# GpSimd's sums of x and output bias and the x2 store take other places in a fused cross-attention and expert kernel

## What is computed

```python
wq = (layernorm(x) @ wq_w.T + wq_b); wk = (ctx @ wk_w.T + wk_b); wv = (ctx @ wv_w.T + wv_b)
probs = softmax(einsum('bthd,bshd->bhts', wq, wk) / sqrt(16))
attn = einsum('bhts,bshd->bthd', probs, wv)
x2 = x + attn @ wo_w.T + wo_b
xt = layernorm(x2); xhat = layernorm(xt); top1 = argmax(xt @ Wg.T)
out = x2 + gelu((xhat * ln_scale[top1] + ln_bias[top1]) @ W1[top1] + b1[top1]) @ W2[top1] + b2[top1]
```

## Time and profile before

| | us |
|---|---|
| three runs, median | 1463.2 |
| lowest and highest run | 1460.85, 1465.98 |
| profiled execution, its own time | 1460.63 |
| its span, first to last instruction | 1458.4 |
| TensorE busy in the span | 1412.0 |
| VectorE busy | 1172.7 |
| ScalarE busy | 872.4 |
| GpSimd busy | 465.0 |

### The profile page before, as it was taken

One profiled execution on the slowest core, in us unless ns is written; L12 is line 12 of the kernel. 1 busy time (PEld: TensorE's weight loads), 2 busy tenths in 40 slices (PEclk: granted clock), 3 DMA queues, 4 the chain that ended last, 5 costly groups with the idle time before them and its releaser, 6 DMA issues.

```text
span 1458.4 us, 39587 instructions
## 1 busy us (share of the span) xinstructions
PE 1412.0 (97%) x15438; PEld 1206.9 (83%) x15438; DVE 1172.7 (80%) x2880; ACT 872.4 (60%) x1451; POOL 465.0 (32%) x602
## 2 busy tenths in 40 slices
PE   6899999999999999999999999989999999999998
PEld 5788888888888888888888888868888888888887
DVE  4788888888888888888888888777777777777775
ACT  5577776777777777777777677653343434333342
POOL 4223332232223223332323233223343434334340
PEclk8899999999999999999999999999999999999999
DMA  7566656665566556756675666412212222222211
GB/s 186 122 170 178 176 158 158 175 173 161 158 166 176 161 161 170 178 150 170 171 176 143 168 172 172 134 34 87 84 61 74 72 73 73 73 73 72 75 59 44
DMA packets 150480, 190.89 MB, mean 131 GB/s; under 512 B 17631, under 2 KB 101146, under 8 KB 150298
## 3 DMA queue, kind: packets, MB, share of 16 engines
q1 hardware_dynamic: 150298, 188.38, 47.5%
HBM read 53.01 MB, written 33.55 MB: 59 GB/s over the span
## 4 chain that ended last, share of the span: by engine, by line
PE 81%; DVE 14%; issue 3%; ACT 1%; DMA 0%; POOL 0%; SPq 0%; ACTq 0%; DVEq 0%
PE st_ps L1252 13%; PE s_ps L1233 12%; PE pp_ps L1110 9%; PE pp_ps L1083 7%; PE pv_ps L1058 7%; PE st_ps L1044 6%; PE s_ps L1016 6%; PE pp_ps L1118 6%; DVE negmax L747 6%; PE pv_ps L1066 4%; DVE cT_lo L773 3%; PE s_ps L1240 2%; PE pp_ps L1199 2%; DVE negmax_wide L750 2%; PE pp_ps L1104 2%
## 5 line engine op out<-in xcount | busy, mean ns | idle before, releaser
L747 DVE TENSOR_REDUCE negmax<-s_ps 128x8 f32<-128x1024 f32 x256 | 311.4, 1216 | 23.0 <-PE s_ps L1016 23.0
L594 ACT ACTIVATE pT<-st_ps 128x1024 f32<-128x1024 f32 x256 | 262.9, 1027 | 106.0 <-PE st_ps L1044 105.0
L1252 PE MATMUL st_ps<-w_hi,q_packed 128*128 128x256 f32 x1024 | 215.9, 296 | 0.2
L1252 PEld LDWEIGHTS st_ps<-w_hi,q_packed 128*128 128x128 f32 x1024 | 167.9, 189 | 10.3 <-issue 5.9
L472 POOL TENSOR_TENSOR xb<-xin,bo_all 128x256 f32<-128x256 f32 x128 | 90.8, 731 | 263.1 <-DMA x_scratch<-xb 170.6
L1233 PE MATMUL s_ps<-k_packed,w_hi 128*128 128x512 f32 x512 | 171.5, 423 | 0.6 <-ACT pT L648 0.6
L1016 PE MATMUL s_ps<-k_packed,q_packed 96*128 96x128 bf16 x2048 | 158.3, 220 | 9.7 <-DVE negmax L747 5.8
L460 POOL TENSOR_TENSOR q_parts<-q,q_parts 128x1024 bf16<-128x1024 f32 x32 | 68.5, 2140 | 298.2 <-ACT q_parts L588 298.2
L1044 PE MATMUL st_ps<-q_packed,k_packed 98*128 98x128 bf16 x2048 | 158.3, 220 | 0.0
L637 ACT ACTIVATE offhotT<-pv_ps 96x512 bf16<-96x512 bf16 x31 | 18.4, 592 | 222.9 <-PE pv_ps L1220 222.9
L1016 PEld LDWEIGHTS s_ps<-k_packed,q_packed 96*128 96x128 bf16 x2048 | 128.3, 98 | 27.8 <-DVE negmax L747 17.8
(11 more groups left out here) (181 smaller groups left out, 3492.9 us busy)
## 6 DMA issues: line engine op xcount, KB each, us to landing
q_packed<-q_parts SPq DMA_DIRECT2D x192, 256.0 KB, 3.9
k_packed<-k_parts SPq DMA_DIRECT2D x192, 256.0 KB, 4.4
xin<-in_x_dram SPq DMA_DIRECT2D x32, 512.0 KB, 3.9
cin<-in_ctx_dram SPq DMA_DIRECT2D x32, 512.0 KB, 4.0
x_scratch<-xb SPq DMA_DIRECT2D x32, 512.0 KB, 4.5
xin<-x_scratch SPq DMA_DIRECT2D x32, 512.0 KB, 3.9
out_dram<-xb SPq DMA_DIRECT2D x32, 512.0 KB, 2.9
q_packed<-negmaxT SPq DMA_DIRECT2D x128, 8.0 KB
```

The lines of the kernel that those rows point to most:

```text
L594: a.activation(pT[u % 2][:], st_ps[:], ACT.Exp, scale=DH ** -0.5).then_inc(s_exp, 1)
L747: v.tensor_reduce(own, s_ps[:].rearrange("p (h s) -> p h s", s=P), AX_X, ALU.max, negate=True).then_inc(s_red, 1)
L1252: t.matmul(o, h[n % 2][:, m, tok].bitcast(F32R), w[:, m, :].bitcast(F32R), start=(m == 0 and k == 0), stop=False)
```

## The change

On the sync queue, `store_x2(g - 1)` is issued ahead of `load_max(g, 2)` and of the packs of parts 1 and 2 of k of the next group; it stood behind all of these. On GpSimd, the first two sums wait until the seventh maxima of the running group have their two parts, and the last two until the eighth have; the waits for s_nrm and s_tl go. Each wait is there for all groups but the first. The wait for the landed store is kept. Work, buffers and the number of DMAs stay as they are.

```diff
@@ sync: group(g)
                     pack(g + 1, 0, 1)
                     pack(g + 1, 0, 2)
                     pack(g + 1, 1, 0)
+                if g > 0:
+                    store_x2(g - 1)
                 load_max(g, 2)
                 if g < LAST:
                     pack(g + 1, 1, 1)
-                if g < LAST:
                     pack(g + 1, 1, 2)
-                if g > 0:
-                    store_x2(g - 1)
                 load_max(g, 3)
@@ gpsimd: residual(n)
                 wait(pool, st_x2[n % 2], (n // 2) * 16)
                 for b in range(GB):
-                    if b == 0 and n > 0:
-                        pool.wait_ge(s_nrm, at(GB, n - 1, 2))
-                    if b == 2 and 0 < n < LAST:
-                        pool.wait_ge(s_tl, at(4, n + 1, 3))
+                    if b % 2 == 0 and n > 0:
+                        pool.wait_ge(s_mp, at(UNITS, n - 1, 7 + b // 2))
                     last = g.tensor_tensor(xb[n % 2][:, b, :], xin[n % 2][:, b, :], bo_all[:], ALU.add)
                 last.then_inc(s_xb, 1)
```

## The result

| | before | changed |
|---|---|---|
| median of four runs beside each other, us | 1462.34 | 1478.35 |
| lowest and highest, us | 1460.85, 1465.98 | 1475.84, 1481.03 |
| profiled execution's span, us | 1458.4 | 1475.9 |
| TensorE busy, us | 1412.0 | 1417.6 |

The changed kernel is slower: its time is 1.0111 times that of the kernel before, 95% interval 1.0097 to 1.0124, that is some 16 us. Its profile has the same work in it and other waits. First TensorE's waits over the whole span (total us, times, longest), to be read beside the earlier trace rows; the changed kernel's lines stand three lower, so L1013, L1080, L747 and L770 are the L1016, L1083, L750 and L773 of before.

The account below looks back on a forecast made before the run. TensorE, busy 97% of the span, was taken as the bound, so only its waits count. Profiled 1460.6 us + 24 for late k packs - 9.7 for the sums = 1474.9, stated as 1476.5 us toward the runs' median; range 1457 to 1494.

Parts of the forecast that it names:

- place B: Start of the sixth step: next group's first scores wait for packed q and k; 24 us loss forecast, bounds 3 and 48.
- Place A: Seventh step: TensorE waits for VectorE's cT_lo ahead of the output projection, 12.4 us in 30 waits.
- The sums' gain: GpSimd's four sums move ahead, off VectorE's small operations, shortening the cT_lo wait: 9.7 us, bounds 5.4 and 12.4.
- rival D: Sums do not move because the store lands only at 709: 24 us slower, 1487 us; chance 3%.
- ordinary groups: 21 groups without a slow store: TensorE stands 0.4 us each before the next group's first scores.
- slow store: Nine groups whose store takes 1.3 us more than the median to land: 1.7 us loss each.
- the delay: Last pack of k comes later behind the early store: 0.8 us taken, from estimates of 0.6 to 1.2 us.
- the slack: Room between the last k pack's landing and the next group's first scores: 0 to 0.9 us, 0.4 taken.
- Rival A: Packs of k have room, so nothing is lost at the first scores and the gain stays: 1453.5 us; chance 13%.
- B: Rival, both small: packs delayed by the issue's 0.65 us only, 10 us against 9.7: 1463 us; chance 14%.
- C: Rival: store slow in most groups, load_max(g, 2) misses the transposed scores, sums' hold added: 1498 us; chance 8%.
- The rule weighed: Whether GpSimd's sums hold VectorE's plain two-SBUF-input L750; if not, the sums' move would be worth nothing.

Follow-up runs that it names:

- e3: Kernel before with a third xb buffer and the sums' new waits, store still behind the packs: 1451.25 us against 1461.97, ratio 0.9928.
- e1: Kernel before with only the sums' new waits, the x2 store kept behind the packs of k: 1462.21 us against 1461.97, ratio 0.9998.
- e8: Changed kernel with a third xb buffer: ratio 1.0098 to the kernel before.
- e5: Kernel before with 128 KB of the x2 store ahead of load_max(g, 2), the rest behind the packs, old sum waits: 1463.43 us against 1461.42.
- e4: Changed kernel with the x2 store behind load_max(g, 2), still ahead of the last three packs of k: 1500.36 us against 1461.97.

## Why the prediction was right, point by point

The forecast was 1476.5 us, measured were 1478.35 us: slower, by the mechanism that was named. Its terms fared differently, and two errors at place B cancelled in part.

**Place A.** The sums' gain was put at 9.7 us. The wait for cT_lo fell by 7.5 us; the sixth and seventh steps are shorter by 0.08 + 0.26 = 0.34 us a group, 10 us. e3 gives 10.7 us as a whole. What stays of the wait is more than the 0.09 us that was forecast: 0.19 us in each of 26 groups. The bound was set by ScalarE's cT_hi, and the rows show another:

```profile
695.68 0.59 ACT L554 CAST cT_hi<-pp_ps 128x512 fp32r<-128x512 f32 x1 [0.38 <-PE pp_ps L1101]
...
696.32 0.17 DVE L749 TENSOR_TENSOR negmax_wide<-negmax,negmax_wide 128x8 bf16<-128x8 f32 x1
696.40 0.68 DVE L770 TENSOR_TENSOR cT_lo<-pp_ps,cT_hi 128x512 fp32r<-128x512 f32 x1
```

cT_hi ends at 696.27 and cT_lo starts at 696.40, right behind VectorE's own L749. It comes 0.72 us behind the start of cT_hi; before it was 0.81 us (713.92 - 713.11), so 0.09 us went in this group and not 0.18. The mean gain of 0.34 us a group goes with longer holds in other groups: before, the two small operations of the sixth step took 0.77 us together on the mean, 0.43 more than unheld, where this group lost 0.27.

**The landing as a condition.** That the sums move only when the store lands early (rival D's condition) holds: e1 is 0.9998. The store lands a little earlier than I took from the page's 4.5 us: 688.11 - 683.88 = 4.2 us from its issue to the first sum in the group shown. The sums then lie over L747 and L749 of the fifth step; in 20 of 29 groups the two take over 0.6 us together, in place of 0.34. The prediction named this, costed it at 0 because of the wait beside it, and e8 bears that out.

**Place B, the sum.** 24 us were forecast and 27 measured (30 x 0.91), but the make-up was wrong. I had 0.4 us in 21 ordinary groups and 1.7 us in nine with a slow store; the start of the scores moved by 0.83 us in the former and by 1.07 us in the latter, so that 17 and 10 us stand where 8 and 15 were forecast. The nine stores that were slow behind the packs land 3.1 to 4.2 us after their issue ahead of them, no slower than the others: the 1.3 us that the sum added for each was not there. That the total fits is partly luck.

**Place B, its two parts.** The terms that were mis-sized are the delay, put at 0.8 us, and the slack, put at 0.4 us. The last pack lands 1.14 us later (18.29 and 19.43 us into the group), and the room was 0.24 us; the difference is the 0.90 us by which the scores move. Of the delay 0.48 us are there when the packs are issued, and 0.66 us come on top with the store's data. The two add up, where the prediction took a little more than one of them. Rival A's argument against itself, "the issue alone already costs 0.65", is wrong twice: the issue takes 0.38 us at this place and makes the packs 0.48 us late, and with 128 KB ahead about as much late issue moved the scores by 0.14 us only (e5), because the room takes up the rest. Behind that the price is steep: 2, 7, 22 us.

**The other rivals.** A (1453.5 us) and B (1463 us) did not come. Both needed a delay not much above the slack; a quarter of the store (e5) comes near that, 2 us slower with the old waits of the sums. C did not come as described: in the changed kernel TensorE's waits behind load_max(g, b) are 0.4 us in all. But a store one place later is as slow as C said, 1500 us, by another mechanism.

**The rule weighed.** The row had sided with the Trainium skill's "GPSIMD Engine Reference", section Specifications (two SBUF inputs contend with GpSimd) against "Advanced Engine Details and Errata", section VectorE Performance Modes, which names only two-port instructions. e3 agrees: with the sums away from them the small tensor_tensor operations take 0.17 us, and the kernel is 10.7 us faster.

## What to carry to other kernels

A transfer that is moved ahead to free a buffer early is paid for by whatever is queued behind it. Ask for the first transfer behind it that someone waits for. Its delay is the later issue plus what the data moved ahead need beyond the idle time of the DMA engines just there; set against it the time between its landing and its reader's start. Here a third buffer gave the whole gain (0.9928) without touching the queue. Where a part of a transfer is ready earlier than the rest, issuing that part in an idle stretch brings two thirds of it (0.9954).

A short operation of VectorE with two SBUF inputs is held to the end of a GpSimd operation that it meets; a row of 0.44 or 0.66 us where its like takes 0.17 shows it. Count such a hold only where the next thing on VectorE doesn't wait for another engine anyway.

## What was not expected of the hardware

In one group of e4 TensorE waited 2.14 us for the packs, and its granted clock fell behind that wait from 2.4 to 1.2 GHz. TensorE's rows, and busy time by stretch (the third last column is the granted clock):

```profile
735.91 0.61 PE L1013 MATMUL s_ps<-k_packed,q_packed 96*128 96x128 bf16 x8 [2.14 <-issue]
...
736.98 1.06 PE L1101 MATMUL pp_ps<-ident,xn 128*128 128x128 f32 x4
```

```profile
733.80:735.90 2.10, 0.00 (x0) 0.02 (x1) 0.68 (x2) 0.00 (x0) 1.36 (x2) 1.00 0.05 16
735.90:737.00 1.10, 1.09 (x17) 1.10 (x18) 0.45 (x1) 0.00 (x0) 0.00 (x0) 0.81 0.36 89
737.00:738.00 1.00, 1.00 (x7) 1.00 (x6) 0.94 (x2) 0.78 (x1) 0.00 (x0) 0.50 0.93 325
...
740.00:742.00 2.00, 2.00 (x47) 1.72 (x46) 1.76 (x4) 0.59 (x1) 0.00 (x0) 1.00 0.00 0
```

The four transposes of L1101 take 1.06 us here and 0.60 to 0.66 us where the clock is at 2.4 GHz. Three groups of e4 had this, behind waits of 1.83, 2.14 and 1.20 us, with sixth steps of 3.63, 3.21 and 3.56 us in place of 1.99: some 4 us in all, which is the rest of e4's 22 us. It did not follow the longest wait of e4 at this place, 2.29 us, nor any in the changed kernel, where they reach 1.5 us; what decides between them the runs do not show.
